# Output bias as a TensorE row, operand splits at other steps, and rows normalised first, in a gated cross-attention and mixture-of-experts block

## What is computed

```python
# attention: queries from LN(x); keys and values from LN(x) and from the context; 8 heads of 64
x = x + tanh(g_xattn) * (softmax(q @ k.T * 64**-0.5) @ v @ Wo + bo)
# feed-forward on y = LN(x): 8 experts, the two best gates count, and one shared expert
comb = softmax(top2(y @ gate_w + gate_b))
out = sum_e comb[:, e] * (gelu(y @ w1[e] + b1[e]) @ w2[e] + b2[e]) + gelu(y @ ws1 + bs1) @ ws2 + bs2
x = x + tanh(g_ffn) * out
```

## Time and profile before

| | us |
|---|---|
| three runs | 156.92, 157.61, 157.63; median 157.61 |
| the profiled execution: its own time | 157.16 |
| the profiled execution: span, first to last instruction | 155.4 |
| PE busy in the span | 141.2 (91%) |
| ACT busy | 118.7 (76%) |
| DVE busy | 107.5 (69%) |
| POOL busy | 96.6 (62%) |

### The profile page before, as it was taken

How to read it: one execution, slowest core, us unless ns; L and a number is a source line. 1 busy time by engine, 2 the same in 40 slices (tenths; PEclk the granted TensorE clock), 3 DMA queues, 4 the chain that set the end, 5 groups by cost and what they waited for, 6 DMA issues and landing times.

```text
span 155.4 us, 4456 instructions
## 1 busy us (share of the span) xinstructions
PE 141.2 (91%) x1836; PEld 108.8 (70%) x1836; DVE 107.5 (69%) x219; ACT 118.7 (76%) x198; POOL 96.6 (62%) x85
## 2 busy tenths in 40 slices
PE   7779699699879899898989789999999999999992
PEld 5424354257536566575767679999999999989992
DVE  0779898679897988997875164537643779896631
ACT  3566789999887897879896989967557598968720
POOL 5504988799999596777969967000300089688730
PEclk9999999999999999999999999999999999999999
DMA  4699950400000000000000000044000000000001
GB/s 144 199 314 305 336 151 0 125 14 4 4 0 2 4 0 4 0 4 0 4 0 4 0 4 0 4 135 139 0 0 6 2 0 10 28 0 4 0 0 34
DMA packets 10253, 7.71 MB, mean 50 GB/s; under 512 B 1101, under 2 KB 8442, under 8 KB 10234
## 3 DMA queue, kind: packets, MB, share of 16 engines
q1 hardware_dynamic: 10234, 7.44, 15.9%
HBM read 7.18 MB, written 0.26 MB: 48 GB/s over the span
## 4 chain that ended last, share of the span: by engine, by line
PE 61%; DVE 20%; ACT 10%; issue 4%; DMA 2%; SPq 0%; DVEq 0%; ACTq 0%
PE banks L1273 12%; PE banks L993 10%; PE banks L995 9%; PE banks L994 9%; DVE part L818 8%; ACT prob L636 4%; DVE wf L922 3%; PE banks L1172 3%; PE banks L1174 3%; DVE k_both L801 3%; PE banks L1173 3%; PE banks L1122 2%; DMA wf<-in_ctx_dram 2%; ACT v_hi L625 2%; PE banks L1140 1%
## 5 line engine op out<-in xcount | busy, mean ns | idle before, releaser
L538 POOL TENSOR_TENSOR p_lo<-prob,p_hi 128x1024 f16<-128x1024 f32 x23 | 49.5, 2158 | 9.7 <-ACT p_hi L644 9.6
L707 ACT ACTIVATE prob<-banks,b1T 128x256 f32<-128x256 f32 x72 | 28.2, 475 | 9.4 <-PE banks L995 9.3
L818 DVE TENSOR_REDUCE part<-banks 128x2 f32<-128x1024 f32 (+1 forms) x24 | 29.0, 1215 | 1.1 <-PE banks L1095 1.0
L636 ACT ACTIVATE prob<-banks 128x1024 f32<-128x1024 f32 x24 | 24.5, 1022 | 6.8 <-PE banks L1140 6.7
L644 ACT ACTIVATE p_hi<-prob 128x1024 f16<-128x1024 f32 x24 | 25.4, 1057 | 0.8
L557 POOL TENSOR_TENSOR k_both<-prob,k_both 128x1024 f16<-128x1024 f32 x8 | 17.0, 2130 | 4.3 <-ACT k_both L715 3.2
L993 PE MATMUL banks<-x2h,wf 128*128 128x256 f16 x72 | 19.6, 273 | 0.0
L1273 PE MATMUL banks<-ring,prob 128*128 128x128 f32 x160 | 19.6, 276 | 0.0
L995 PE MATMUL banks<-x2h,wf 128*128 128x256 f16 x72 | 19.6, 273 | 0.0
L994 PE MATMUL banks<-x2h,wf 128*128 128x256 f16 x72 | 19.6, 272 | 0.0
L1172 PEld LDWEIGHTS banks<-v_hi,p_hi 128*128 128x128 f16 x192 | 17.4, 98 | 2.8 <-issue 2.5
(11 more groups left out here) (156 smaller groups left out, 329.3 us busy)
## 6 DMA issues: line engine op xcount, KB each, us to landing
ring<-in_L_ffn_w_dram SPq DMA_DIRECT2D x16, 256.0 KB, 4.0
wf<-in_ctx_dram SPq DMA_DIRECT2D x2, 256.0 KB, 5.1
ring<-in_L_xattn_Wk_dram SPq DMA_DIRECT2D x2, 256.0 KB, 4.4
ring<-in_L_xattn_Wv_dram SPq DMA_DIRECT2D x2, 256.0 KB, 5.8
ring<-in_L_ffn_ws_dram SPq DMA_DIRECT2D x2, 256.0 KB, 5.7
x_sb<-in_x_dram SPq DMA_DIRECT2D x1, 256.0 KB, 2.9
ring<-in_L_xattn_Wq_dram SPq DMA_DIRECT2D x1, 256.0 KB, 4.7
ring<-in_L_xattn_Wo_dram SPq DMA_DIRECT2D x1, 256.0 KB, 6.6
```

The source lines that it names most:

```text
L538: nc.gpsimd.tensor_tensor(p_lo[:, u % RINGP, :, :].rearrange("p a n -> p (a n)"), prob[:, u % RINGE, :], p_hi[:, u % RINGP, :, :].rearrang ...
L636: nc.scalar.activation(prob[:, u % RINGE, :], units(u).rearrange("p a n -> p (a n)"), ACT.Exp, scale=DH ** -0.5 / S_SCORE).then_inc(exp_do ...
L707: nc.scalar.activation(hid[:, k % NHID, c * T1:(c + 1) * T1], span(2 * (k % 2), HC * T1)[:, c * T1:(c + 1) * T1], ACT.Gelu, bias=b1T[:, e ...
L818: nc.vector.tensor_reduce(dst, src, AX_X, ALU.max).then_inc(part_done, 1)
```

## The change

- `bo` is no longer added to x. It is loaded as one row of one partition (`bo_row`), later in SP's list, and PE adds it as a last product into each of the two tiles of `TAIL_WO`: the row of constants `unit_row` (memset once by POOL) against `bo_row`, float32, a contraction over one row. POOL's five instructions of step 3 and DVE's wait for them are gone.
- The split of `WO` moves from steps 1 and 2 to `WO_STEP` = 12 (ACT) and 13 (POOL).
- `EARLY` falls from 5 to 4. The early splits of experts 1 to 3 move from steps 4 to 12 to steps 14 to 22, and only expert 0 still has its w2 split early. w1 of expert 4 and w2 of expert 1 join the late ones. The late steps are dealt out anew.
- For w2 of experts 5 to 8 POOL makes `hi` instead of ACT (`late_hi`, steps in `W2P_STEP`).
- In the ramp DVE normalises the rows before the `lo` of the context.
- PE waits for `bo_row` and for one more constant before `TAIL_WO`; SP's load of expert 8 also waits for the `lo` of w2 of expert 1, whose slot it takes.

```diff
-EARLY = 5
-EARLY_HI_STEP = (4, 6, 8, 10)
-EARLY_LO_STEP = (6, 8, 10, 12)
-W1_STEP = {5: FFN0, 6: FFN0 + 1, 7: FFN0 + 4, 8: FFN0 + 5}
-W2_STEP = {2: FFN0 + 2, 3: FFN0 + 3, 4: FFN0 + 6, 5: FFN0 + 7, 6: FFN0 + 8, 7: FFN0 + 9, 8: FFN0 + 10}
+EARLY = 4
+EARLY_HI_STEP = (14, 17, 20)
+EARLY_LO_STEP = (16, 19, 22)
+WO_STEP = 12
+W1_STEP = {4: FFN0, 5: FFN0 + 1, 6: FFN0 + 3, 7: FFN0 + 5, 8: FFN0 + 6}
+W2_STEP = {1: FFN0 + 2, 2: FFN0 + 4, 3: FFN0 + 7, 4: FFN0 + 8}
+W2P_STEP = {5: FFN0 + 4, 6: FFN0 + 5, 7: FFN0 + 6, 8: FFN0 + 8}
...
-            return 2 if j < 2 else 1
+            return 2 if j == 0 else 1
...
                     sp.wait_ge(y_ps, j - RING + 1)
+                    if j > RING:
+                        sp.wait_ge(w2_lo, j - RING)
...
-            sp.dma_start(bo_sb[:, :], bo.partition_broadcast(P)).then_inc(ld_bo, 16)
             load_a(WV2)
...
             sp.dma_start(ctx_sb[1], ctx_d[1]).then_inc(ld_ctx[1], 16)
+            sp.dma_start(bo_row[:, :], bo.rearrange("(a n) -> a n", a=1)).then_inc(ld_bo, 16)
...
+            nc.gpsimd.memset(unit_row[:, :], S_ACTV * S_W).then_inc(consts, 1)
...
+            def late_hi(j):
+                pool.wait_ge(ld_f[j], 32)
+                nc.gpsimd.tensor_tensor(wf[:, 0, EORDER[j], 1, :], ring_f(j)[:, 1, :],
+                                        c_sw[:, :].broadcast_to([P, 512]), ALU.mult).then_inc(w2p_hi, 1)
...
-                if i == 2:
+                if i == WO_STEP + 1:
                     lo_by_pool(WO)
-                if i == 3:
-                    add_bias()
...
-                if i == 1:
+                if i == WO_STEP:
                     scaled_for_pool(WO)
...
-                if item[0] == "tx":
-                    normalise_rows(x_sb, 0, NT, 1)
...
             row_statistics(x_sb, 0, NT)
+            normalise_rows(x_sb, 0, NT, 1)
...
+                for j in W2P_LATE:
+                    if W2P_STEP[j] == i - 1:
+                        dve.wait_ge(w2p_hi, W2P_LATE.index(j) + 1)
+                        expert_lo(j, slice(1, 2)).then_inc(w2p_lo, 1)
...
-                            last = three(misc[:, q * D:(q + 1) * D], (oT[:, 0, t, cols], oT[:, 1, t, cols]),
-                                         w_pair(WO, cols), start=(c == 0), stop=(c == INNER // P - 1))
+                            three(misc[:, q * D:(q + 1) * D], (oT[:, 0, t, cols], oT[:, 1, t, cols]),
+                                  w_pair(WO, cols), start=(c == 0), stop=False)
+                        last = nc.tensor.matmul(misc[:, q * D:(q + 1) * D], unit_row[:, :], bo_row[:, :],
+                                                start=False, stop=True)
```

More of the change, by code:

```diff
@@ L67 @@
 BIAS_STEP = 13
-EARLY = 5
-EARLY_HI_STEP = (4, 6, 8, 10)
-EARLY_LO_STEP = (6, 8, 10, 12)
-W1_STEP = {5: FFN0, 6: FFN0 + 1, 7: FFN0 + 4, 8: FFN0 + 5}
-W2_STEP = {2: FFN0 + 2, 3: FFN0 + 3, 4: FFN0 + 6, 5: FFN0 + 7, 6: FFN0 + 8, 7: FFN0 + 9, 8: FFN0 + 10}
-W1_LATE, W2_LATE = list(W1_STEP), list(W2_STEP)
+EARLY = 4
[5 more added lines that the diff above has]
+W2P_STEP = {5: FFN0 + 4, 6: FFN0 + 5, 7: FFN0 + 6, 8: FFN0 + 8}
+W1_LATE, W2_LATE, W2P_LATE = list(W1_STEP), list(W2_STEP), list(W2P_STEP)
 TAIL_O0, TAIL_O1, TAIL_WO, TAIL_X, TAIL_GATE, TAIL_COMB, TAIL_B2 = TAIL_STAGES = range(7)
@@ L266, in block_kernel @@
         gb = sb("gb", [P, E], F32)
-        bo_sb = sb("bo_sb", [P, D], F32)
+        bo_row = sb("bo_row", [1, D], F32)
+        unit_row = sb("unit_row", [1, P], F32)
         gates = sb("gates", [P, 4], F32)
@@ L331, in block_kernel @@
         tanh_done = sem("tanh_done")
-        xb_done = sem("xb_done")
         w_hi, w_lo = sem("w_hi"), sem("w_lo")
@@ L358, in block_kernel @@
         w2_hi, w2_lo = sem("w2_hi"), sem("w2_lo")
+        w2p_hi, w2p_lo = sem("w2p_hi"), sem("w2p_lo")
         h_ps = sem("h_ps")
@@ L546, in _ @@
                     early_lo(0)
-                if i == 2:
+                if i == WO_STEP + 1:
                     lo_by_pool(WO)
-                if i == 3:
-                    add_bias()
                 if i in EARLY_HI_STEP:
                     early_hi(EARLY_HI_STEP.index(i) + 1)
+                for j in W2P_LATE:
+                    if W2P_STEP[j] == i:
+                        late_hi(j)
                 k = i - FFN0 - 1
@@ L872, in tail @@
                 elif s == TAIL_WO:
-                    dve.wait_ge(xb_done, NT)
                     dve.wait_ge(scales_done, 2)
@@ L1186, in tail @@
                     wait_split(pe, WO)
+                    pe.wait_ge(ld_bo, 16)
+                    pe.wait_ge(consts, 9)
                     for q in range(QT):
@@ L1264, in _ @@
                             pe.wait_ge(w2_lo, W2_LATE.index(k % NE) + 1)
+                        if k % NE in W2P_LATE:
+                            pe.wait_ge(w2p_lo, W2P_LATE.index(k % NE) + 1)
                         pe.wait_ge(hl_done, hid_splits(k))
```

## The result

| | before | after |
|---|---|---|
| median (us) | 157.45 (156.92 to 157.63) | 158.71 (158.58 to 158.86) |
| the profiled execution: its own time, span | 157.16, 155.4 | 158.69, 156.9 |
| ratio to before | 1 | 1.0079, interval 1.0048 to 1.0110 |

What follows compares the result with a forecast made beforehand. PE was taken as the bound: full in the feed-forward part, 3.5 us idle from 43.7 to 91.3. Terms 0.4 - 1.2 - 0.8 - 0.4 - 0.2 + 1.2 = -1.0 us, from 157.61, gave 156.6 us; range 155.8 to 159.0.

Steps and rivals of the forecast that it cites:

- The ramp, +0.4: At the start, DVE idles until about 6.38 instead of beginning at 5.99, so all work behind ends 0.4 us later.
- `WO`, -1.2: At step 1, ACT's two passes no longer precede step 2's exponential: 1.2 us won; at step 12 they cost 0 to +0.4.
- The early `lo`s, -0.8, -0.4, -0.2: PE's waits behind early `lo`s in steps 7, 10 and 15 shrink or go: 0.8, 0.4 and 0.2 us won.
- The late splits, 0: The redealt late `hi`s and `lo`s on DVE, ACT and POOL cost nothing, all three having over 16 us to spare.
- The bias, +1.2: Four float32 products in the tails at steps 19 and 28 cost PE 0.3 us each, 1.2 in all, between 0.9 and 1.4.
- The collisions: DVE's `lo` held behind POOL's `p_lo`: +1.5 us at step 16, +0.7 at step 19; one alone 157.3 or 158.1, chance 0.17.
- The rival: At steps 16 and 19 both `lo`s are held by POOL at the SBUF, +2.2 us: 158.8 us, chance 0.25.
- POOL's queue: Argument against POOL coming first at step 16: its queued work ends at 71.4; 0.1 us later, DVE gets in first.

Runs made afterwards that it cites:

- the three timed pairs: Changed kernel, kernel before and fastest version, each timed with old and new DVE order in the ramp; the pairs differ by 0.06, 0.18 and 0.38 us.
- the fastest version: Changed kernel with early `lo`s of experts 1 and 2 at steps 10 and 13, bias on POOL at step 7, old ramp order: 154.53 us.
- The kernel with both races won: Changed kernel with the `lo`s of steps 16 and 19 one instruction earlier on DVE, ahead of `nmax`: 156.88 us.

## Why the prediction was wrong

**The ramp, +0.4.** In the profile +0.41, by the mechanism named. But the term rested on one landing of the context; the three timed pairs show 0.06 to 0.38.

**`WO`, -1.2.** Right, here -1.20 at step 2, alone -1.25, and step 12 cost nothing by step 15.

**The early `lo`s, -0.8, -0.4, -0.2.** Right: -0.74 by step 8, -0.56 from there to step 12 (exponential 12 at 58.58, before 60.67), -0.18 to step 16; together -1.48 for -1.4. What stayed is what the text named: PE's waits of 0.53 us for a row maximum (at 61.45, 69.59 and 79.19 us), which stood in the kernel before too.

**The late splits, 0, and POOL's `hi`s.** Right: PE has no gap in the feed-forward part, and the fastest version, which has them too, needs 64.05 us for 64.06.

**The bias, +1.2.** The mis-sized term: 1.95, beyond its bound of 1.4. The row taken as nearest has two products of nine rows back to back, 0.32 each. A single one among products over 128 rows pays the change of rows on both sides and adds 0.41 to 0.51. The text said that each stands alone among float16 products, and then took the low value. Even without any collision the sum would have been 0.4 - 1.2 - 1.4 + 1.95 = -0.25. The kernel with both races won is this case: its span is 155.1 us, 0.3 below the 155.4 of before, and its median 156.88, 0.5 below.

**The collisions: the step that decided the sign.** The forecast let both `lo`s pass unheld; in the run both were held. The rival was right in rule and place, and at step 16 in price: +1.5 forecast and 1.49 measured. At step 19 it had +0.7 beside a bias of 0.6, 1.3 in all; 1.28 were measured, but as 0.36 beside a bias of 0.92. What failed was who comes first. The rows put POOL first at both, and against that I set POOL's queue, estimated to be free at 71.4, 'the very moment': if 0.1 us late, DVE would win. The queue was free in time: the `p_lo` began at 71.30, 0.08 us behind its `p_hi`, and DVE came at 71.36, so the distance is the 0.06 of the rows. In the run with only the first `lo` moved POOL is idle before that `p_lo`, and it begins 0.08 us behind its `p_hi` there too (70.38 + 1.06 = 71.44, then 71.52). The queue came within 0.1 us of mattering, which is chance, and no estimate good to 0.1 us could have told. But both rows said POOL, the queue argument did not reach step 19, and a cost of 2.2 us hanging on 0.06 should have had more than 0.25 for both. That the two events are not independent was missed as well. At steps 16 and 19 the distance is the same in every profile that has this order: `nmax` starts 0.01 to 0.02 us before the `p_lo` (before: 73.56 and 73.58, 81.67 and 81.69), and a `lo` right behind it 0.06 or 0.07 after (71.30 and 71.36, 80.90 and 80.97, 79.62 and 79.69). At the earlier pairs of heads it is not (63.14 and 63.97).

**The whole.** Between the spans of the two profiles lie 0.41 - 1.20 - 1.48 + 1.48 + 1.29 + 1.0 = +1.5 us, where the forecast had -1.0. Of these 2.5 us, 1.48 are lost at step 16, 0.69 at step 19 (1.29 less the 0.6 that the bias was given there) and 0.4 in the feed-forward part. That the rival's 158.8 lies within 0.1 us of the result is partly luck: its sum was +1.2, with the bias too small, but it was counted from 157.61, and every later median of the kernel before is 0.2 to 0.3 us lower (157.34 to 157.45).

## What to carry to other kernels

Before a DVE instruction with two SBUF inputs is moved, look at what POOL starts within its length: here coming second cost it 1.93 us of the 2.13 of POOL's instruction, coming first cost it nothing and POOL 0.4, and one place up in the list decided it. Two delays that end at the same wait do not add, so an undo of one shows less than its price, and the last culprit found looks free until the other is gone. A product over one row in PE's stream costs more than its columns: read its price at a change of shape, not from a row of equals.

## What the runs showed of the hardware

I had not expected that a product over one row in the midst of products over 128 would add 0.1 us at either side, so that two float16 products of 128 columns, 0.07 us apart, add 0.31; the change from 128 to 64 rows costs the same 0.1. I had not expected either that a DVE instruction held by one POOL instruction gets in ahead of the next of POOL's queue (1.34 us, then 2.60 for the `p_lo`; at step 16, 2.61 us, then 1.49 for POOL's `hi`, which takes 1.04 elsewhere). And the landing of the same transfer at the start moved by up to 1.0 us between profiled executions (PE's transposes of the context start at 4.45 to 5.47 us and end at 5.1 to 6.1), which is as much as the terms of this sum.
